# Head attention on one core: v fetched dense and spread by GpSimd, TensorE's loop moved to another place in its instruction blocks, a round's two projections taken apart

## The reference, cut to what matters

```python
b, h, w, c = x.shape                       # 8, 56, 56, 128
xs = x.reshape(b, h * w, c)
q, k, v = xs @ Wq.T, xs @ Wk.T, 2 * (xs @ Wv.T)
q, k, v = (t.reshape(b, n, HEADS, DIM_HEAD) for t in (q, k, v))   # 8 heads of 16
q, k, v_h = _l2norm(q), _l2norm(k), _l2norm(v)
attn_head = softmax(einsum('bnhd,bngd->bnhg', v_h, v_h))          # 8 x 8 for each token
q = einsum('bnhg,bngd->bnhd', attn_head, q)
k = einsum('bnhg,bngd->bnhd', attn_head, k)
attn = softmax(einsum('bnhd,bnhe->bnde', k, q))                   # 16 x 16 for each token
out = einsum('bnhd,bnde->bnhe', v, attn)                          # then the projection
```

## Time and profile before

| | before |
|---|---|
| three runs | 3550.62, 3564.91, 3569.99 us (median 3564.91) |
| the profiled execution | 3554.55 us, its span 3552.8 us |
| PE busy in the span | 3015.3 us (85%) |
| DVE, ACT, POOL busy | 1937.6, 1269.4, 567.8 us |
| granted TensorE clock, mean of the span | 0.913 |
| first scores of `attend` | at 2044.6 us |
| TensorE's loop of `attend`, rounds 3 to 101 | 2074.2 to 3315.7 us |
| scores of the last unit | from 3410.2 us |

### The profile page before, as it was taken

The page is one execution under the profiler, slowest core; times in us unless marked ns, Lnnn a source line. Parts: engine busy times, 40 slices in busy tenths (PEclk is TensorE's granted clock), DMA queues, the critical chain, the costliest instruction groups (busy, mean ns, idle before and its releaser), DMA issues. The chain is left out here.

```text
span 3552.8 us, 145120 instructions
## 1 busy us (share of the span) xinstructions
PE 3015.3 (85%) x62769; PEld 2232.1 (63%) x62769; DVE 1937.6 (55%) x3276; ACT 1269.4 (36%) x2841; POOL 567.8 (16%) x473
## 2 busy tenths in 40 slices
PE   5776989999999999999989677777777777776779
PEld 4553488666666666666644265666666666665679
DVE  4553533666666666666657555455455455454533
ACT  3554443222222222222234344343344343444300
POOL 0000020222222222222211211111111111111100
PEclk7887989999999999999989899888888788888989
DMA  6874000111111111111189444444444444444446
GB/s 151 241 227 127 1 1 1 39 46 44 44 45 45 45 45 44 45 45 45 45 334 397 174 81 74 65 74 66 73 64 76 66 74 66 74 71 70 73 102 206
DMA packets 1033184, 320.17 MB, mean 90 GB/s; under 512 B 872433, under 2 KB 1018414, under 8 KB 1028654
## 3 DMA queue, kind: packets, MB, share of 16 engines
q1 hardware_dynamic: 711058, 182.69, 23.6%
q10 hardware_dynamic: 321692, 130.88, 13.5%
HBM read 157.66 MB, written 155.75 MB: 88 GB/s over the span
## 5 line engine op out<-in xcount | busy, mean ns | idle before, releaser
L845 DVE TENSOR_TENSOR terms<-spec,ps_z 112x456 f32<-112x456 f32 x1024 | 575.5, 624 | 403.2 <-PE ps_z L728 403.1
L738 PEld LDWEIGHTS ps_q<-inv_w,prod 112*57 112x57 f32 x16384 | 450.9, 133 | 174.1 <-issue 172.2
L738 PE MATMUL ps_q<-inv_w,prod 112*57 112x56 f32 x16384 | 484.4, 217 | 0.8 <-DVE prod L851 0.8
L1166 PE MATMUL ps_s<-v_blocks 128*64 128x64 f32 x6272 | 276.6, 257 | 223.5 <-issue 162.1
L728 PE MATMUL ps_z<-x_half,fwd_w 120*112 120x456 f32 x1024 | 458.8, 571 | 0.0
L826 POOL TENSOR_TENSOR prod<-terms 112x456 f32<-112x456 f32 x256 | 297.5, 1162 | 1000.4 <-DVE terms L845 1000.4
L783 ACT ACTIVATE q_half<-ps_q 121x448 f32<-121x448 f32 x255 | 138.8, 544 | 827.3 <-PE ps_y L746 827.3
L1166 PEld LDWEIGHTS ps_s<-v_blocks 128*64 128x64 f32 x6272 | 254.2, 169 | 241.1 <-issue 195.0
L1129 POOL TENSOR_TENSOR k_blocks<-k_mixed,same_of 128x896 f32<-128x896 f32 x112 | 188.1, 1679 | 1185.2 <-ACT k_mixed L1277 1185.2
L1339 DVE TENSOR_TENSOR e_blocks<-s_exp,same_of 128x896 f32<-128x896 f32 x112 | 122.2, 1091 | 364.9 <-ACT s_exp L1262 364.9
L1177 PE MATMUL ps_l<-q_mixed,k_blocks 32*64 32x64 f32 x12544 | 280.3, 247 | 40.1 <-issue 39.1
(11 more groups left out here) (135 smaller groups left out, 4237.5 us busy)
## 6 DMA issues: line engine op xcount, KB each, us to landing
qk_heads<-st_qk ACTq DMA_DIRECT2D x56, 476.0 KB
qk_rows<-qk_heads SPq DMA_DIRECT2D x112, 238.0 KB, 5.0
conv_in<-v_sb ACTq DMA_DIRECT2D x112, 224.0 KB, 3.3
v_in<-conv_in SPq DMA_DIRECT2D x512, 49.0 KB
conv_out<-y_sb ACTq DMA_DIRECT2D x512, 49.0 KB
y<-conv_out SPq DMA_DIRECT2D x8, 1792.0 KB, 12.7
v_blocks<-v_heads SPq DMA_DIRECT2D x896, 14.0 KB, 3.0
x_in<-in_x SPq DMA_DIRECT2D x8, 1568.0 KB, 9.4
```

Source lines behind the costliest of these rows:

```text
L738: last = pe.matmul(ps_q[64 * ri:64 * ri + NF, c * SIDE:(c + 1) * SIDE], prod[b % 2][:, x, c * NF:(c + 1) * NF], k.inv_w[:, x, ri * SIDE:(r ...
L845: last = dve.tensor_tensor(terms[b % 2][:, x, :], k.spec[0:NFFT, s, bass.ds(c * CC, CC), :].rearrange("p c f -> p (c f)"), ps_z[b % 2][z][ ...
L1166: last = pe.matmul(to, vb[m][:, g, a, :], vb[m][:, g, a, :], start=True, stop=True)
```

## The change

Five things are done at once:

- `v_dense`: four new buffers (NV = 4) take v of two units as it lies in DRAM, by eight DMAs for each two units (before: eight for each unit). They wait for GpSimd to have read the buffer, not for TensorE.
- `spread_v`: GpSimd multiplies each run of 8 heads with a constant 0/1 pattern (`slot8`) into `v_blocks`, 1,792 elements a partition for each unit. It stands behind `spread_k(i)` for unit i+2, and waits for `outputs(i-1)`. The three clearing memsets of `v_blocks` go.
- `load_qk(u)` waits for `o_r` of unit u-3, and its arrival is waited for at `mix`, no longer at `scores`; scores wait for `spread_v`.
- TensorE's projection of the first half stands ahead of `logits`, that of the second half behind it. ScalarE's `copy_in` of the first half stands ahead of `exp_l`.
- 80 semaphore increments that nothing waits for stand ahead of TensorE's first instruction in `attend`.

```diff
+            def load_v(n):
+                if n >= NB:
+                    return
+                if n >= NV:
+                    sp.wait_ge(vb_r, 2 * (n - NV) + 2)
+                sp.wait_ge(st_stored[n % 2], 32 * (n // 2 + 1))
+                v = t.VT[n * 2 * UT:(n + 1) * 2 * UT].rearrange("(x a q) (d h) -> a q d x h", q=4, a=2, h=HEADS)
+                for a in range(2):
+                    for q in range(4):
+                        sp.dma_start(vd[n % NV][64 * a + q:64 * a + 64:4], v[a, q]).then_inc(v_loaded[n % NV], 16)
+            def load_qk(u):
                 m, n = u % RING, u // 2
                 if u < RING:
-                    sp.wait_ge(cleared, m + 1)
+                    sp.wait_ge(cleared, 1)
                 else:
-                    sp.wait_ge(o_ps, u - RING + 1)
+                    sp.wait_ge(o_r, u - RING + 1)
                 sp.wait_ge(st_stored[n % 2], 32 * (n // 2 + 1))
...
+            load_v(0)
             for u in range(NU):
-                turn(u)
+                load_qk(u)
                 load_xn(u + AU + 1)
+                if u % 2 == 0:
+                    load_v(u // 2 + 1)
...
+            def spread_v(u):
+                n, g0 = u // 2, u % 2 * 2 * GU
+                if u % 2 == 0:
+                    pool.wait_ge(v_loaded[n % NV], 128 * (n // NV + 1))
+                if u >= RING:
+                    pool.wait_ge(o_ps, u - RING + 1)
+                pool.tensor_tensor(vb[u % RING][:].rearrange("p g r (m h) -> p (g r) m h", h=HEADS),
+                                   bcast(vd[n % NV][:, g0:g0 + 2 * GU], 2, 8),
+                                   bcast(k.slot8[:].rearrange("p (m h) -> p m h", h=HEADS), 1, 2 * GU), ALU.mult).then_inc(vb_r, 1)
...
             for i in range(NU):
                 spread_k(i)
+                if i + 2 < NU:
+                    spread_v(i + 2)
...
             def round_of(c, j):
                 i = c * RING + j
                 if unit(i):
-                    scores(i, j, c + 1)
+                    scores(i, j)
+                if unit(i + AU):
+                    project(i + AU, (j + AU) % RING, c + (j + AU) // RING + 1, 0)
                 if unit(i - 1):
                     logits(i - 1)
                 if unit(i + AU):
-                    for x in range(2):
-                        project(i + AU, (j + AU) % RING, c + (j + AU) // RING + 1, x)
+                    project(i + AU, (j + AU) % RING, c + (j + AU) // RING + 1, 1)
                 if unit(i):
-                    mix(i, j)
+                    mix(i, j, c + 1)
...
+            for _ in range(80):
+                pe.sem_inc(aligned, 1)
...
+                if unit(i + AU):
+                    copy_in(2 * (i + AU))
                 if unit(i - 1):
                     exp_l(i - 1)
-                if unit(i + AU):
-                    copy_in(2 * (i + AU))
```

More of the change, by code:

```diff
@@ L1043, in attend @@
     RING = 3
+    NV = 4
     LOOPED = (NU - AU) // RING
@@ L1062, in attend @@
         vb = [sb(f"v_blocks{m}", [128, GU, 2, 64]) for m in range(RING)]
+        vd = [sb(f"v_dense{m}", [128, 4 * GU, HEADS]) for m in range(NV)]
         qk = [sb(f"qk_rows{m}", [128, GU + 1, QKW]) for m in range(RING)]
@@ L1077, in attend @@
         st_stored = [sem(f"st_stored{m}") for m in range(2)]
-        in_loaded = [sem(f"in_loaded{m}") for m in range(RING)]
-        cleared, k_r, qkv_ps, qkv_read = sem("cleared"), sem("k_blocks_ready"), sem("qkv_ps"), sem("qkv_read")
+        v_loaded = [sem(f"v_dense_loaded{m}") for m in range(NV)]
+        qk_loaded = [sem(f"qk_loaded{m}") for m in range(RING)]
+        cleared, vb_r, k_r, qkv_ps, qkv_read = sem("cleared"), sem("v_blocks_ready"), sem("k_blocks_ready"), sem("qkv_ps"), sem("qkv_read")
         nsq_r, nsc_r, nrm_r, rn_r, st_r, vn_r = (sem(n) for n in ("nsq_ready", "nsq_clamped", "nrm_ready", "rnorm_ready", "st_ready", "v_norm_ready"))
@@ L1083, in attend @@
         l_ps, l_exp, z_r, zi_r, p_r = (sem(n) for n in ("l_ps", "l_exp_ready", "z_ready", "z_inv_ready", "p_ready"))
-        o_ps, o_r, mix_seen = sem("o_ps"), sem("o_ready"), sem("mix_seen")
+        o_ps, o_r, mix_seen, aligned = sem("o_ps"), sem("o_ready"), sem("mix_seen"), sem("loop_aligned")
         block = ctx.enter_context(nc.Block())
@@ L1098, in load_xn @@
                 sp.dma_start(xn[w % RING][:], t.XN[b, :, c * UT:(c + 1) * UT]).then_inc(xn_loaded[w % RING], 16)
[L1100 to L1101 removed]
+            def load_v(n):
[9 more added lines that the diff above has]
+            def load_qk(u):
                 m, n = u % RING, u // 2
                 if u < RING:
[L1104 removed]
+                    sp.wait_ge(cleared, 1)
                 else:
[L1106 removed]
+                    sp.wait_ge(o_r, u - RING + 1)
                 sp.wait_ge(st_stored[n % 2], 32 * (n // 2 + 1))
[L1108 to L1115, removed]
+                sp.dma_start(qk[m][:, 0:GU, :], t.QK[u * UT:(u + 1) * UT].rearrange("(g n) h x -> (n h) g x", n=16)).then_inc(qk_loaded[m], 16)
             for w in range(AU + 1):
                 load_xn(w)
+            load_v(0)
             for u in range(NU):
[L1120 removed]
+                load_qk(u)
                 load_xn(u + AU + 1)
+                if u % 2 == 0:
+                    load_v(u // 2 + 1)
         @block.gpsimd
@@ L1136, in copy_norm @@
                 pool.tensor_copy(st_qk[a][:, :, :, QKM], nrm[a][:, :, 16:24]).then_inc(vn_r, 1)
+            def spread_v(u):
[7 more added lines that the diff above has]
+                                   bcast(k.slot8[:].rearrange("p (m h) -> p m h", h=HEADS), 1, 2 * GU), ALU.mult).then_inc(vb_r, 1)
             for m in range(RING):
-                pool.memset(qk[m][:, GU:, :], 0.0)
-                pool.memset(vb[m][:], 0.0).then_inc(cleared, 1)
+                last = pool.memset(qk[m][:, GU:, :], 0.0)
+            last.then_inc(cleared, 1)
             for n in range(AHEAD - 1):
                 copy_norm(n)
+            spread_v(0)
+            spread_v(1)
             for i in range(NU):
                 spread_k(i)
+                if i + 2 < NU:
+                    spread_v(i + 2)
                 if i % 2 == 0 and i // 2 + AHEAD - 1 < NB:
@@ L1157, in project, with scores @@
                           start=True, stop=True).then_inc(qkv_ps, 1)
-            def scores(i, m, loads):
-                pe.wait_ge(in_loaded[m], loads * 144)
+            def scores(i, m):
+                pe.wait_ge(vb_r, i + 1)
                 if not isinstance(i, int) or i:
@@ L1179, in logits, with mix @@
                 last.then_inc(l_ps, 1)
-            def mix(i, m):
+            def mix(i, m, loads):
+                pe.wait_ge(qk_loaded[m], loads * 16)
                 pe.wait_ge(e_r, i + 1)
```

6 lines of the change are left out of this document (4 added, 2 removed).

## The result

The changed kernel takes 3373.57 us (median of 4 runs, 3368.56 to 3377.82), the kernel before 3566.11 us beside it. The ratio is 0.9467, with a 95% interval of 0.9436 to 0.9498: faster by 5.3%. The prediction was 3295 us with a range of 3160 to 3430.

The account below looks back on a forecast made before the run. Instruction fetch and the return of v were taken to bound rounds of 12.54 us, VectorE contention afterwards. Saving 99 x (12.54 - 10.0) = 251: 3554.55 - 251 - 17 + 2 = 3288, predicted as 3295 us, range 3160 to 3430.

Parts of the forecast that it names:

- fetch: Attention loop reaches into an eighth instruction block and is refetched each pass; aligned, 2.24 us of issue pauses a round go.
- contention: GpSimd's spread_v holds VectorE instructions with both inputs in SBUF; rounds of 9.4 to 10.25 us instead of 8.6.
- the round of 10.0 us: Forecast length of an attention loop round after the change: middle 9.8 us plus 0.2 for the clock, against 12.54 before.
- the return of v: Chain from outputs through SyncE's v issues and qk_rows to later scores: 11.5 us, taken as nearly a round's bound.
- The clock's part: TensorE's granted clock in the attention loop was to rise from 0.86 to 0.95 or more once fetch stops go.
- The rival by which the loop is fetched anew all the same: Eight or nine packets a pass stay, each jump back costs 4 us; 11.6 us a round, 3447 us; chance 0.12.
- the floor that the prediction gives: TensorE's 7.96 us of work a round plus 0.63 us of outputs waiting for p_norm: 8.6 us.
- nearer operation: spread_v priced after k_blocks, the same multiply with spread inputs, at 3.2 us; line 826 would make it 4.6.
- the two branches of the odd round: Rounds with st_v: 9.0 us if st_qk and st_v precede spread_v, 10.7 if it comes between; even rounds 9.8.
- The list of four VectorE instructions: Instructions with both inputs in SBUF, expected to be held by GpSimd: mask, p_norm, st_qk and, every other round, st_v.
- I count them as nothing: The 80 increments run while TensorE waits for its first input; 4 us if that cover were missing.
- The rounds behind the loop: Nine rounds after the attention loop: from 10.5 us each to 8.6, 17 us saved.

Follow-up runs that it names:

- e1: The changed kernel without the 80 increments: 3614.75 us, ratio 1.0149 to the kernel before.
- e11: The kernel before with qk_rows on its own semaphore, waited for at mix, and no padding: 3554.18 us, ratio 0.9977.
- e2: The kernel before with the 80 increments and nothing else: 3249.63 us, ratio 0.9126.
- e6: As e4, with spread_v written as two instructions of half the size: 3215.18 us, ratio 0.9024.
- e7: As e2, with qk_rows on a semaphore of its own, waited for at mix and not at scores: 3133.0 us, ratio 0.8800.
- e4: The changed kernel, but in odd rounds GpSimd waits with spread_v until st_v is done: 3344.42 us, ratio 0.9388.
- e8: As e7, with the 80 increments in tens behind TensorE's first eight units of projections: 3121.73 us, ratio 0.8771.
- e3: The changed kernel with both projections behind the logits again and the first copy_in behind exp_l: 3364.5 us, ratio 0.9447.
- e10: As e2, with an added GpSimd multiply of spread_v's size and place that nobody reads, v on its old path: 3371.49 us, ratio 0.9465.

## Why the prediction was right, and where it was not

The time lies in the range, and fetch and contention were the right causes, but part of the closeness is luck. Two errors inside the round of 10.0 us point in opposite directions, and a third, on the return of v, never reached the sum. Against the profiled execution the sum was 3288 us, and 3377.8 were measured. The miss of 90 us is made up of 51 in the loop (99 x 0.52), 11 behind it, 9 of the increments, 8 in the start of the stage and 11 that lie ahead of it.

**Fetch: right.** The place of the loop in the blocks, worked out from where TensorE paused, decides. 295 packets became 7 with the padding in either kernel, came back in e1, and were 294 in e11. The clock's part was half right: it rose from 0.86 to 0.92 and not to 0.95. Behind the waits for the mask in the long rounds the outputs ran at the lower level (3.01 us). The mean of the loop is 0.96 in e2 and 1.00 in e6 and e7. The rival by which the loop is fetched anew all the same has fallen. The Trainium skill, Runtime: NRT & Kernel Launch, "Instruction fetch mechanics", says that a taken branch whose target is outside the current window of two pages forces a fetch of the target's page; by it every pass of this loop would fetch at least once, in all of these kernels. Seven packets in 33 passes disagree, and the measurement decides. What was run are loops that begin 0, 2 or 69 (convolve) and 176 or 178 instructions into a block. That the step lies exactly between seven blocks and eight fits all of them, but no start in between was tried.

**The return of v: the step that failed.** The prediction took 11.5 us from outputs to "the scores of the next unit but one" as the bound of a round, and wrote that this chain "is hardly shorter than the 12.54 us of a round". The chain runs from the end of one round's outputs to the scores two rounds on. Between those scores and the ones two rounds earlier lie one round of work, 7.6 us, and the chain: (11.5 + 7.6) / 2 = 9.6 us a round, and e2 shows 18.0 us for the two rounds above. The change was credited with removing a bound of 11.5 that stood at 9.4. The forecast did not fall with it, because its sum was built on what bounds the kernel afterwards. But it hid the main lesson: with fetch gone, the new path of v could win at most 9.4 - 8.6 = 0.8 us a round down to the floor that the prediction gives, and a semaphore for qk_rows won 1.2 (9.38 to 8.21, e7).

**Contention on VectorE: right in kind, too small in size.** Forecast 10.0 us a round, measured 10.52. Two terms were mis-sized. spread_v was priced at 3.2 us after k_blocks, the "nearer operation"; it takes 4.2 in place and 4.0 free of VectorE (e4), which is 2.2 ns an element, between k_blocks' 1.9 and line 826's 2.5. And of the two branches of the odd round I took the middle, where the worse one came in 47 of 49: spread_v goes ahead of st_v. 10.7 us was worked out for it; with 1.0 more for spread_v it is 11.7, measured about 12.0. The other round was better than thought (mostly 8.7, not 9.8), because there st_qk is through when outputs end and is not held. The list of four VectorE instructions was short by one: `clamp` is held too (2.85 us in e4), which the changed kernel shows in only 2 of 49 rounds, since there st_v takes the hold. st_v's 4.47 us and the 4.07 of st_qk in e4 last to the end of spread_v, and in e6 VectorE gets in between two instructions. The Trainium skill, SBUF — State Buffer, "Who interferes with whom", calls the shared ports an exclusive lock and says, of VectorE's two-port modes, that the engine that comes first has them for the whole instruction and the other fully blocks; these durations agree, for instructions with two inputs in SBUF as well.

**The increments: "I count them as nothing".** They cost 9.0 us at the start: the first projection comes 12.5 us behind SyncE's first load instead of 3.5 (2033.0 and 2020.5 now, 2013.3 and 2009.8 before; in e1, without them, it is 2.1). The cover was shorter than the 80 increments. e8 removes the cost by placing them in real waits.

**The rounds behind the loop: too hopeful.** 8.6 us forecast, 9.8 measured (88.6 over 9), with GpSimd busy for 53.8 us there and the clock at 0.90. The mask is held there too (2.31 us in the median of the nine), and mix waits for it; I had left the contention out of this term. The saving was 6 us and not 17. Rounds 0 to 2 and the way to the first scores cost 10 us more beside the increments, where 2 were expected.

**Projections apart:** the forecast counted 0.63 us a round for outputs that wait for p_norm, as the price of the shorter cover. The waits are there (35.3 us in all, 0.36 a round), but they are there in e3 too, with the projections together (40.8 us), and not in the kernel before (0.3 us) or in e2. So they come with spread_v, not with the split: p_norm stands behind the late mask in VectorE's queue. What the split costs in a kernel without spread_v was not run.

**What stays open.** e10 shows that the contention is enough for the 122 us between e2 and the change. That the new path of v is then worth about nothing holds for rounds that the mask bounds; with the spread in halves (e6) the kernel is 34 us faster than e2, and how much of that is the path of v was not taken apart. Dense v was not run by itself, since something must spread it. Why st_qk slips ahead of spread_v in most rounds of the changed kernel and not in e4 is read from the order in the traces and not tested.

## What to carry to other kernels

When several edits come together, time each alone: here one of the five parts brought the whole gain, and the largest edit cost about two fifths of it. A chain through a ring of buffers bounds the number of rounds it spans, together with the work inside them; divide before calling it a round's bound. Before work is moved to GpSimd, list VectorE's instructions with both inputs in SBUF, and look in a trace for others that are held (here `clamp`). If it must go there, cut it into short instructions: that gave 129 us (e4 to e6). Letting one late VectorE instruction go first gave 29, because the next ones were held in its place. For a long TensorE loop, count where its ends fall in the blocks of 256 instructions that its pauses show, and put the padding where the engine waits anyway.

## What was not expected of the hardware

- One edit of 80 increments, with no work in them, is worth 312 us of 3562 (e2): a loop of 1,728 instructions was fetched with 8.9 packets of 16 KB a pass in one place, and with 7 packets in all 33 passes in another.
- The same GpSimd work costs more as one instruction than as two: spread_v whole (4.0 us, e4) makes rounds of 10.25 us and in halves (2.08 us at least, 2.25 in the median, e6) rounds of 8.94, although GpSimd is busy for longer with the halves.
- A VectorE instruction with a single input, `clamp`, is held by GpSimd as well: 0.21 us in the kernel before, 2.86 in the median of e4's loop.
- GpSimd's own small copies (0.24 us in the kernel before) take up to 1.1 us in the changed kernel. The one below follows the mask of 2508.74 that is shown above, and both end within 0.1 us of each other, at 2511.3 and 2511.2. The hold works both ways:

```profile
2510.20 1.11 POOL L1146 COPY st_qk<-nrm 112x32 f32<-112x32 f32 x1
```
